# Sixteen rows of one gather fetched by single-row transfers from SyncE, in a two-layer graph network kernel

## The reference, cut to what matters

```python
h = relu(layernorm(x))
# layer 0
m = relu(concat(h[src], edge16) @ w1a + b1a) @ w1b + b1b
agg = segment_sum(m, dst) / max(count(dst), 1)
x = x + relu(concat(h, agg) @ w2a + b2a) @ w2b + b2b
h = relu(layernorm(x))
# layer 1
x = x + (1 + eps) * h + segment_sum(relu(h[src] + edge32), dst)
```

## Time and profile before

| what | value |
|---|---|
| median of three runs | 7352.49 us (7350.89 to 7363.88) |
| profiled execution, span | 7360.0 us |
| PE matmul busy | 6429.2 us, 87% |
| PEld weight load busy | 5436.7 us, 74% |
| POOL busy | 4564.4 us, 62% |
| ACT busy | 4370.5 us, 59% |
| DVE busy | 3791.4 us, 52% |
| mean granted TensorE clock | 0.917 of full |

### The profile page before, as it was taken

How to read it: one execution, slowest core, us unless ns; L and a number is a source line. 1 busy time by engine, 2 the same in 40 slices (tenths; PEclk the granted TensorE clock), 3 DMA queues, 4 the chain that set the end, 5 groups by cost and what they waited for, 6 DMA issues and landing times. The chain is left out here.

```text
span 7360.0 us, 107042 instructions
## 1 busy us (share of the span) xinstructions
PE 6429.2 (87%) x32834; PEld 5436.7 (74%) x32835; DVE 3791.4 (52%) x9052; ACT 4370.5 (59%) x8707; POOL 4564.4 (62%) x4834
## 2 busy tenths in 40 slices
PE   7888888888888888888887888888888889888888
PEld 5777777777777777777777777777777777777777
DVE  5343434434444443434446666666666666666666
ACT  5555555555555555555556666666666666666665
POOL 5666666666666666666655666666666666666665
PEclk8999899888898999898998999999999999999999
DMA  3222221222222122222211111111111111111111
GB/s 104 55 55 55 54 54 54 55 55 55 55 56 54 54 55 55 54 54 57 56 44 43 42 44 44 44 39 44 44 42 41 44 44 42 41 44 44 44 39 40
DMA packets 331462, 367.43 MB, mean 50 GB/s; under 512 B 87161, under 2 KB 256536, under 8 KB 331166
## 3 DMA queue, kind: packets, MB, share of 16 engines
q0 software_dynamic: 152000, 160.05, 10.0%
q1 hardware_dynamic: 46276, 130.67, 5.3%
q10 hardware_dynamic: 133146, 76.25, 3.7%
HBM read 358.17 MB, written 8.46 MB: 50 GB/s over the span
## 5 line engine op out<-in xcount | busy, mean ns | idle before, releaser
L1015 PE MATMUL bank<-part_high,owner_hot 125*128 125x448 f32 (+1 forms) x10500 | 4250.6, 405 | 224.1 <-issue 162.9
L1015 PE MATMUL bank<-part_low,owner_hot 125*128 125x448 f32 (+1 forms) x10500 | 4127.5, 393 | 152.6 <-issue 150.9
L986 POOL DMA_INDIRECT gathered<-projected_rows,indices x2500 | 2366.8, 947 | 1412.8 <-issue 705.7
L986 POOL DMA_INDIRECT gathered<-hidden_rows,indices x2250 | 2135.2, 949 | 1277.1 <-issue 854.6
L1015 PEld LDWEIGHTS bank<-part_high,owner_hot 125*128 125x128 f32 x10500 | 2144.2, 204 | 505.2 <-issue 228.8
L1015 PEld LDWEIGHTS bank<-part_low,owner_hot 125*128 125x128 f32 x10500 | 2137.9, 204 | 412.6 <-issue 189.7
L1118 ACT ACTIVATE owner_hot<-owner_in,minus_piece 125x256 fp32r<-125x256 f32 (+2 forms) x3948 | 1591.4, 484 | 128.4 <-remote 69.9
L1261 DVE SCALAR_TENSOR_TENSOR hidden<-window_f,places_now,bank 128x512 f32<-128x512 f32 x1500 | 1104.8, 737 | 1074.6 <-remote 609.0
L1123 ACT ACTIVATE owner_hot<-owner_hot 125x1792 fp32r<-125x1792 f32 (+1 forms) x750 | 1275.5, 1701 | 23.8
L1317 DVE TENSOR_TENSOR sums<-sums,bank 97x48 f32 (+1 forms) x1250 | 244.2, 195 | 1694.6 <-remote 1396.7
L1045 PEld LDWEIGHTS bank<-hidden,messages 128*97 128x97 f32 x6250 | 644.4, 170 | 424.2 <-issue 418.3
(11 more groups left out here) (128 smaller groups left out, 2721.4 us busy)
## 6 DMA issues: line engine op xcount, KB each, us to landing
owner_in<-owner_rows SPq DMA_DIRECT2D x188, 448.0 KB
edges<-in_edge ACTq DMA_DIRECT2D x124, 400.0 KB
gathered<-projected_rows,indices POOLq DMA_INDIRECT x2500
gathered<-hidden_rows,indices POOLq DMA_INDIRECT x2250
hidden<-owner_rows SPq DMA_DIRECT2D x62, 448.0 KB
edges<-in_edge ACTq DMA_DIRECT2D x124, 200.0 KB
projected_rows<-projected SPq DMA_DIRECT2D x25, 168.0 KB
sources<-in_src_cols SPq DMA_DIRECT2D x1, 1562.5 KB, 6.4
```

The source lines that it names most:

```text
L986: pool.indirect_dma_start(gathered_rows(k, row)[:, t, :], None, table, bass.IndirectOffsetOnAxis(ap=index(k, odd(turn))[:, t:t + 1], axis= ...
L1015: last = nc.tensor.matmul(bank[pick_home[home]][:, 0:PITCH * D].rearrange("p (f b) -> p f b", b=PITCH)[:, :, 0:rows.shape[2]], pick_hot(pi ...
```

## The change

In each turn and in both layers, tile 0 of slot 2 is gathered with 112 rows (partitions 0 to 111). The other 16 rows (partitions 112 to 127) are fetched by SP, with 16 transfers of one row each. For that SP loads the 16 row numbers into a small tile `single_sources` (one transfer, two turns ahead), loads them into 16 of its registers, waits until the slot's buffer is free, and issues the 16 transfers, whose source address is taken from a register. DVE waits for these in `add_edges` of slot 2, on one semaphore more. SP's loop has two turns in its body in both layers; in each turn stand in this order the owner load, the load of row numbers for two turns on, and the 16 rows of the next turn.

```diff
+SINGLE_SLOT, SINGLE_TILE = 2, 0
+SINGLES = 16
...
+        single_sources = sb("single_sources", [1, 2, SINGLES], I32)
...
+                    def load_single_sources(turn):
+                        chunk = SLOTS * number(turn) + SINGLE_SLOT
+                        with nc.allow_non_contiguous_dma(reason="one index from each of the last partitions' rows"):
+                            sp.dma_start(single_sources[0:1, odd(turn), :],
+                                         src_cols[P - SINGLES:P, bass.ds(chunk, 1), SINGLE_TILE].rearrange("p o -> o p")
+                                         ).then_inc(single_sources_in[odd(turn)], 16)
+
+                    def fetch_singles(turn, first=False):
+                        sp.wait_ge(single_sources_in[odd(turn)], 16 * (turn.half + turn.offset // 2) + 16)
+                        sp.sem_inc(singles_listed, 1)
+                        _, loaded = nc.values_load_multi_w_load_instructions(
+                            single_sources[0:1, odd(turn), :], engines=[mybir.EngineType.SP], min_val=0, max_val=N - 1,
+                            skip_runtime_bounds_check_because="a source is the number of a node, as the gathers take it")
+                        if not first:
+                            buffer_free = rectified if layer == 0 else added
+                            sp.wait_ge(buffer_free, chunks_before(turn) + (SINGLE_SLOT + 1))
+                        for n in range(SINGLES):
+                            p = P - SINGLES + n
+                            sp.dma_start(gathered_rows(SINGLE_SLOT, row)[p:p + 1, SINGLE_TILE, :],
+                                         table[bass.ds(loaded[n], 1), :]).then_inc(singles_in, 16)
+
+                    load_single_sources(FIRST)
+                    load_single_sources(Turn(0, 1))
+                    fetch_singles(FIRST, first=True)
                     if layer == 0:
-                        with sp.Fori(0, ITERS - 1) as i:
-                            sp.wait_ge(squares_up, NBATCHES * i + NBATCHES)
-                            load_owners(i + 1, owner_in, owners_in[0][0])
+                        def load_next(turn):
+                            sp.wait_ge(squares_up, NBATCHES * number(turn) + NBATCHES)
+                            load_owners(number(turn) + 1, owner_in, owners_in[0][0])
...
+                    with sp.Fori(0, HALVES - 1) as half:
+                        for offset in range(2):
+                            load_next(Turn(half, offset))
+                            load_single_sources(Turn(half, offset + 2))
+                            fetch_singles(Turn(half, offset + 1))
...
+                            rows = P - SINGLES if (k, t) == (SINGLE_SLOT, SINGLE_TILE) else P
                             pool.indirect_dma_start(
-                                gathered_rows(k, row)[:, t, :], None, table,
-                                bass.IndirectOffsetOnAxis(ap=index(k, odd(turn))[:, t:t + 1], axis=0)
+                                gathered_rows(k, row)[0:rows, t, :], None, table,
+                                bass.IndirectOffsetOnAxis(ap=index(k, odd(turn))[0:rows, t:t + 1], axis=0)
                             ).then_inc(gather_in[k], 16)
...
                     def add_edges(k, turn):
                         counts = [16 * tiles_in(k, parity) for parity in range(2)]
                         dve.wait_ge(gather_in[k], before(turn, *counts) + counts[odd(turn)])
+                        if k == SINGLE_SLOT:
+                            dve.wait_ge(singles_in, 16 * SINGLES * number(turn) + 16 * SINGLES)
```

More of the change, by code:

```diff
@@ L738, in sum_near_windows @@
             summed = sem(f"summed{layer}")
+            single_sources_in = [sem(f"single_sources_in{layer}_{parity}") for parity in range(2)]
+            singles_in = sem(f"singles_in{layer}")
+            singles_listed = sem(f"singles_listed{layer}")
             picks = LAYER_PICKS[layer]
@@ L948, in _, with load_next @@
+                    load_single_sources(FIRST)
+                    load_single_sources(Turn(0, 1))
+                    fetch_singles(FIRST, first=True)
                     if layer == 0:
-                        with sp.Fori(0, ITERS - 1) as i:
-                            sp.wait_ge(squares_up, NBATCHES * i + NBATCHES)
-                            load_owners(i + 1, owner_in, owners_in[0][0])
-                    else:
[L953 to L961, removed]
+                        def load_next(turn):
+                            sp.wait_ge(squares_up, NBATCHES * number(turn) + NBATCHES)
+                            load_owners(number(turn) + 1, owner_in, owners_in[0][0])
+                    else:
+                        def load_next(turn):
+                            sp.wait_ge(squares_up, NBATCHES * number(turn) + NBATCHES)
+                            load_owners(number(turn) + 2, owners_of(turn), owners_in[1][odd(turn)])
@@ new lines, in _ @@
+                    with sp.Fori(0, HALVES - 1) as half:
[3 more added lines that the diff above has]
+                            fetch_singles(Turn(half, offset + 1))
+                    load_next(Turn(0, ITERS - 3))
+                    load_single_sources(LAST)
+                    fetch_singles(BEFORE_LAST)
+                    if layer == 0:
+                        load_next(BEFORE_LAST)
@@ L962, in _ @@
+                    fetch_singles(LAST)
                     if layer:
```

## The result

The changed kernel takes 7511.74 us (median of four runs, 7505.87 to 7519.65) against 7354.61 us before (four runs, 7350.89 to 7363.88): ratio 1.0215, interval 1.0202 to 1.0227. It is slower by 157 us. The forecast was 7355 us, and its range ended at 7420.

A forecast was written before the change was run, and what follows sets the result against it. PE was taken as the bound. 7360.0 + 0 (POOL) + 0 (bursts) + 0 (DVE's wait) + 1 (start) = 7361 us profiled; on the median's scale 7352.5 + 1, rounded up to 7355 us, range 7330 to 7420.

The forecast's parts named there:

- What bounds: Whole kernel: PE is the bound, busy 87% of 7360.0 us, with POOL (62%) paced by it.
- POOL's relief: POOL's one 112-row gather a turn: saves nothing to 0.118 us a turn, at most 29.5 us in all; taken as nothing.
- SP's burst at 0.41 us a single: SP's 16 single-row issues: 0.41 us each, 6.5 us a burst; 12.4 us at the slow end.
- the rival: SP's burst outgrows its room before layer 0's owner load, deciding from 1.0 us a single: 7737 us; chance 0.05, milder form 0.10.
- What is queued behind the burst in layer 0: Layer 0's owner load behind SP's burst: 11.3 us of room, 4.8 us of slack; 0 us for 124 turns.
- The point of decision: Layer 0's owner load: the burst reaches ACT only from (11.3 + 4.8)/16 = 1.0 us a single.
- The bursts cost 0: SP's bursts in both layers: hidden before the next owner load and before DVE needs the rows; 0 us.
- the third rival, clock: Timing shifts from DVE's extra wait or later gather landings cost PE some clock: 7371 to 7397 us; chance 0.12.
- the serial rival: SP's singles served one after another on one ring, 36.8 us a turn in both layers: 9375 us; chance 0.01.
- Rows arrive in time, DVE's wait: Slot 2 on DVE: rows land about 17 us early, extra wait hides under a reduction; 0 us, wait at most 19.
- The register load: SP's load of 16 row numbers into registers: up to 3.8 us, inside 19.4 us before the buffer comes free; no cost.
- The start: Before layer 0's loop: turn 0's singles delay the first owner load; 1 us, up to 6.

The follow-up runs named there:

- thin_gathers: Changed kernel with every gather after the first turn cut to 16 rows; 7632.67 us (one run) to 7427.33 before.
- incs96: Kernel before with 96 semaphore increments a turn on SP that nobody waits for, plus the small row-number load, gathers whole; ratio 1.1044.
- after_act: Changed kernel, but in layer 0's loop ACT issues the owner load itself, so it does not stand behind SP's burst; ratio 1.0186 to the kernel before.
- after_again: Changed kernel, unaltered, measured again on another chip beside the follow-up runs; ratio 1.0198 to the kernel before.
- only0: The whole change in layer 0 alone, layer 1 as in the kernel before; ratio 1.0126.
- incs_loop: Kernel before with SP increments nobody waits for, one and then a 16-pass loop of one, plus the small row-number load; ratio 1.0116.
- one_load: Changed kernel with one SP transfer of fixed rows 0 to 15 replacing the 16 singles and their register load; ratio 1.0080 to the kernel before.
- dve_wait: Kernel before with one more, already fulfilled wait on DVE ahead of slot 2's addition; ratio 1.0002.
- aside: Changed kernel's SP burst written to a tile nobody reads, gathers whole, no added DVE wait; ratio 1.0180 to the kernel before.
- incs: Kernel before with 48 semaphore increments a turn on SP that nobody waits for, plus the small row-number load, gathers whole; ratio 1.0105.
- only1: The whole change in layer 1 alone, layer 0 as in the kernel before; ratio 1.0063.
- static_rows: Changed kernel with the 16 singles taken from fixed rows of the table, so hardly any register work; ratio 1.0107 to the kernel before.
- singles8: Changed kernel with 8 singles and a 120-row gather; ratio 1.0117 to the kernel before.
- short_gather: Kernel before with tile 0 of slot 2 gathered with 112 rows, the other 16 not fetched by anyone; ratio 1.0051.
- short4: Kernel before with all gathers of slot 2 cut to 112 rows, the other rows not fetched; ratio 1.0015.

## Why the prediction was wrong

*What bounds.* Right: PE, in both layers, with POOL waiting. POOL's relief was worth nothing. A gather's time is hardly one of rows: the 112-row gather has its median at 0.928 us, the 16-row gather of thin_gathers at 0.837, the whole one at 0.944. That is about 1 ns a row, so that 16 rows less save 0.016 us where the upper bound was 0.118. The row of thin_gathers:

```profile
L1024 POOL DMA_INDIRECT gathered<-projected_rows,indices x2500: 830/837/6174, 62.8 to 4017.5; - x193
```

*SP's burst at 0.41 us a single.* This is the first step that failed. 0.41 is the undisturbed value; about one SP instruction in seven takes 0.7 us in the kernel after (2203 of 15,104), and a single is three instructions. The sum should have carried the mean: 0.87 us in layer 0, above the 0.78 taken as the upper end and just below the 1.0 at which the rival was to decide. The row that said so was quoted: a branch of 3/45/709 ns. I read it as a property of branches (73 of 190 stalled before); but 81 of 494 register operations stalled too.

*What is queued behind the burst in layer 0.* The place was right, the owner load goes out a median 6.2 us late and ACT waits 150.3 us. The point of decision was right too: 14.0 us is past the 11.3 of room and within the 16.1 with the slack, and incs96 at 20.4 us is beyond both and pays 5.6 us a turn. But what the kernel after pays by this road is small: a turn of after_act is 0.07 us shorter than one of after_again and 0.18 shorter than one of only0, 9 to 22 us of 157.

*"The bursts cost 0".* This is the step that decided. I let SP reach the others only through a load that comes late or a row that lands late. The runs show a third way: SP's instruction stream itself lengthens the turn. 48 increments a turn that no engine waits for, with the small load, cost 1.0105, and again 1.0116 from a loop (incs_loop). They cost in layer 1, where no load is late, and there one_load leaves at most 0.07 us of the 0.33 to the rest of SP's additions. In the kernel after most of the loss is idle time of PE, 75 of the 100 us in layer 0's window and 34 of the 40 in layer 1's; under which of PE's waits it stands shifts from kernel to kernel. Some of it can be clock. These are windows of layer 1 in dve_wait and then in aside:

```profile
4060.00:7260.00 3200.00, 2820.56 (x14346) 2447.60 (x14346) 1991.30 (x4896) 2016.59 (x3380) 1993.96 (x2099) 0.94 0.19 42
```

```profile
4060.00:7260.00 3200.00, 2806.37 (x14082) 2444.37 (x14081) 1950.46 (x4801) 1983.28 (x3315) 1948.87 (x2054) 0.92 0.18 42
```

2820.56/14346 = 196.6 ns and 2806.37/14082 = 199.3 ns a matmul; at some 123 matmuls a turn (14346 × 27.47/3200) the 2.7 ns are 0.33 of aside's 0.54 us. But aside is the far end. In the same window incs_loop, incs, after_act, after_again and only1 have 197.5 to 198.1 ns, static_rows and singles8 196.3 and 196.8, and the kernels without a burst there 196.1 to 197.3. In the kernel after layer 1's clock stayed at 0.93 and only 5.8 of 40 us were of this kind. So the third rival, clock, may have something in it, through another door than the one I named; in the kernel after it is the smaller part.

The transfers add to it: aside is 0.75% above incs and, on one chip with it, 0.64% above incs_loop. The Trainium skill (page "DMA: Bandwidth & Descriptors", section "Rules for kernel authors") says to coalesce small transfers. Its direction fits: 16 rows in one transfer have 1.0080 (one_load), 16 transfers from fixed rows 1.0107. The two intervals overlap; layer 1's turn, 27.55 against 27.75 us, says the same. But the serial rival drawn from it did not come: no wait of DVE in the kernel after names the singles (in after_again one does, for 0.2 us). The same page, section "Issuing engines are not separate DMA queues", calls the sequencer's time for starting a transfer usually small relative to the transfer. One issue is, with 0.228 us; that is not the whole price here, since incs starts no singles and has 1.0105.

*Rows arrive in time, DVE's wait.* Right, 0 and 0 (dve_wait 1.0002). *The register load.* 1.24 us for 16 registers, where at most 3.8 was allowed; hidden. *The start.* 1.8 us late, forecast 1, up to 6.

What stays open. What the 0.7 us is, and by what road SP's stream reaches PE, is not settled. It is not the gathers' traffic, not the length of SP's code, not the kind of instruction. PE's own small instructions never stalled (0 of 3430 of 0.66 to 0.73 us, before and after). DVE's and POOL's did a little, 33 of 6564 and 30 of 4120 before and 38 of 6808 and 37 of 4120 after, which is no clear rise. One rival has no run: that the recording of so many SP instructions causes the stalls, and with them the loss. The ratios do not exclude it, since the record gives a span and a granted clock for every run, so that none is known to have gone unrecorded. Also open is layer 0's 0.3 us for one shorter gather (short_gather) that goes with four (short4). It may be in the 1.0080 of one_load. Of the 0.77 us that after_again loses in a turn of layer 0, incs has 0.26 and aside 0.59; the last 0.18 is not assigned. No version tried is faster than the kernel before.

## What to carry to other kernels

An idle engine is not free. Price small instructions on it by the mean, with the maximum column beside the median, and ask what they do to the engine that is the bound even if nobody waits for them: here 0.33 us of a turn for 48 increments and the little around them. To find such a cost, put in the instructions without their work (increments that nobody waits for), and check in each such run that nothing else has come late with them: incs96 was not clean in either layer. And sum an engine's waits before reading one of them: a line that trebles can be an exchange. A wait that newly appears, like ACT's 150 us, is a suspect and not yet a cause: take it away (after_act) and see whether the time follows.

## What the runs showed of the hardware that was not expected

- SP's small instructions (move, register arithmetic, branch, increment, issue of a single) have medians of 17 to 228 ns in the kernel after, but 7 to 15 of 100 of SP's instructions take 0.66 to 0.73 us (105 of 1510 in dve_wait, 2203 of 15,104 in the kernel after), and some up to 1.4 us.
- Increments on SP that nobody waits for lengthen PE's turn: 48 a turn, with one small load, 1.0105 (incs) and in layer 1 0.33 us, of which the load and the rest account for at most 0.07 (one_load).
- An indirect gather takes 0.837 us for 16 rows, 0.928 for 112 and 0.944 for 128. Worked out from these, an estimate: 0.82 us before its first row and 1 ns a row.
- A load of 16 registers takes 1.24 us on SP, hardly more than 1.18 for mostly five on DVE.
